# First graph layer of a two-layer GNN kernel: mask laid out per edge, linear part of the leaky logits as product columns, node sums in two halves, node map moved behind the turned logits, GpSimd made to wait for the mask

## What is computed

```python
h = relu(layernorm(x));  s_n, v_n = equivariant_layernorm(h)
msg = (s_n, v_n) @ W_src [src] + (s_n, v_n) @ W_dst [dst]       # gathered rows
m1_s, m1_v = tensor_product(msg, rsh, rbf @ W_rbf)              # per edge
a = (m1_s @ W_alpha).reshape(e, 4, 16)
a = where(a > 0, a, 0.2 * a)                                    # leaky
a = sum(a * alpha_dot, axis=-1)                                 # 4 logits of an edge
ex = exp(a - segment_max(a, dst));  alpha = ex / (segment_sum(ex, dst) + 1e-16)
val = gated(m1_s @ Ws_val, m1_v @ Wv_val)
m2 = tensor_product(val, rsh, w2);  h2 = m2 @ W_vlin            # 4 heads
out = node + segment_sum(alpha * h2, dst) @ W_p
```

## Time and profile before

| | |
|---|---|
| median of 3 runs | 10570.75 us (10557.51 to 10588.19) |
| the profiled execution, its own time | 10573.21 us |
| its span, first to last instruction | 10571.2 us |
| busy: PE, DVE, POOL, ACT | 80%, 70%, 59%, 31% |
| mean granted TensorE clock | 0.899 of full speed |

### The profile page before, as it was taken

The page is one execution under the profiler, slowest core; times in us unless marked ns, Lnnn a source line. Parts: engine busy times, 40 slices in busy tenths (PEclk is TensorE's granted clock), DMA queues, the critical chain, the costliest instruction groups (busy, mean ns, idle before and its releaser), DMA issues. The chain is left out here.

```text
span 10571.2 us, 201187 instructions
## 1 busy us (share of the span) xinstructions
PE 8497.0 (80%) x50848; PEld 6425.6 (61%) x50849; DVE 7420.9 (70%) x18020; ACT 3241.5 (31%) x8443; POOL 6191.2 (59%) x6291
## 2 busy tenths in 40 slices
PE   1388888888888888888888888877658888888888
PEld 1277777777777777777777777766433333333335
DVE  2477777777777777777777777666237777777775
ACT  0133333333333333333333333322222222222223
POOL 0266666666666666666666666543007777677774
PEclk9599999999999999999999999888558888889889
DMA  2133333333333333333333333222002222222221
GB/s 35 48 83 81 83 83 81 82 83 82 81 85 81 84 83 81 83 83 82 83 82 82 83 81 83 71 61 52 8 12 57 57 57 58 58 57 57 57 57 48
DMA packets 560992, 725.68 MB, mean 69 GB/s; under 512 B 228019, under 2 KB 334899, under 8 KB 560956
## 3 DMA queue, kind: packets, MB, share of 16 engines
q0 software_dynamic: 225792, 385.65, 16.3%
q1 hardware_dynamic: 335164, 339.61, 12.1%
HBM read 708.76 MB, written 16.06 MB: 69 GB/s over the span
## 5 line engine op out<-in xcount | busy, mean ns | idle before, releaser
L739 PE MATMUL bank_pair<-w_msg,blocks 128*128 128x160 f32 (+1 forms) x15640 | 2420.7, 318 | 768.1 <-DVE blocks L983 768.1
L739 PEld LDWEIGHTS bank_pair<-w_msg,blocks 128*128 128x128 f32 x15640 | 2314.5, 219 | 859.3 <-DVE blocks L983 859.3
L1377 POOL DMA_INDIRECT gotf<-f_tab,idx x1568 | 1712.8, 1092 | 748.5 <-issue 383.9
L697 POOL DMA_INDIRECT got_src<-src_tab,idx x1568 | 1520.4, 970 | 726.6 <-POOL idx L691 368.3
L697 POOL DMA_INDIRECT got_dst<-dst_tab,idx x1568 | 1495.8, 954 | 529.3 <-issue 527.5
L761 PEld LDWEIGHTS bank_pair<-weights_t,product 128*128 128x128 f32 x12896 | 1493.9, 194 | 309.1 <-issue 294.9
L761 PE MATMUL bank_pair<-weights_t,product 128*128 128x128 f32 x12896 | 1570.5, 281 | 8.9 <-ACT weights_t L885 8.2
L1417 PE MATMUL bank_pair<-val,to_node 128*128 128x449 f32 x3136 | 1477.3, 619 | 6.0 <-DVE val L1520 6.0
L706 POOL TENSOR_TENSOR edge<-rbf,y 128x512 f32<-128x512 f32 x391 | 661.1, 1691 | 1244.5 <-PE bank_pair L728 1137.5
L894 ACT ACTIVATE weights<-near,small 128x512 f32<-128x512 f32 x391 | 282.2, 722 | 3014.1 <-DVE small L933 3014.1
L1468 ACT ACTIVATE val<-pre,y_edge 128x160 f32<-128x160 f32 x1568 | 542.9, 417 | 1894.1 <-DVE pre L1508 1894.1
(11 more groups left out here) (267 smaller groups left out, 12953.8 us busy)
## 6 DMA issues: line engine op xcount, KB each, us to landing
rbf<-in_rbf SPq DMA_DIRECT2D x392, 256.0 KB
dst_bc<-in_dst_rows SPq DMA_DIRECT2D x391, 256.0 KB
y<-in_y SPq DMA_DIRECT2D x392, 128.0 KB
y<-in_y SPq DMA_DIRECT2D x392, 96.0 KB
got_src<-src_tab,idx POOLq DMA_INDIRECT x1568
got_dst<-dst_tab,idx POOLq DMA_INDIRECT x1568
gotf<-f_tab,idx POOLq DMA_INDIRECT x1568
rbf<-in_rbf SPq DMA_DIRECT2D x392, 32.0 KB
```

The source lines that it names most:

```text
L697: pool.indirect_dma_start(out=buf[slot][:, t, :], out_offset=None, in_=table[:, :], in_offset=bass.IndirectOffsetOnAxis(ap=idx[slot][:, c: ...
L739: return nc.tensor.matmul(to, blocks[rows, k, P * t:P * t + P], w_msg[rows, c0:c1], start=start, stop=stop)
L1377: pool.indirect_dma_start(out=got[k % 2][:, t, :], out_offset=None, in_=f_tab[:, :], in_offset=bass.IndirectOffsetOnAxis(ap=idx[k % 2][:, ...
```

## The change

The mask no longer exists as a 128 x 512 tensor that is added to the turned logits. `keys` holds for every edge the place of its node within the window (computed once, in the set-up). In step g DVE compares 32 node numbers with the keys (`apart`, 128 x 128), multiplies by LEAST (`bar`), and, once the logits of g are there, adds mask and logits while widening them (`widen`, 128 x 512). This replaces ACT's widening. The turned logits then carry the mask: the maximum is a plain `tensor_reduce` of PSUM, and ACT takes the exponentials from PSUM. `far`, `near`, `dst_bc` and its DMA are gone.

The leaky function is split: 0.2 times the sum over a head is linear, so it becomes four more columns of the message product (`w_msg`, 160 to 164 columns in the pieces for scalars), and only 0.8 relu is multiplied and reduced (`bent`); one small addition joins the two.

On PE the sums over edges run in two halves around the second pair of `weigh`, and `project` follows `spread_logits`. Its result is copied by ACT from PSUM to SBUF (`pick`, four instructions), and `take_window` becomes one DVE instruction that reads SBUF alone. `multiply` is split: the vector part stays ahead of `messages(g, 2)`, the scalar part goes behind it, followed by the mask. The two peak updates (L937, L938) become one. POOL's `combine` of g+1 waits until DVE has made the mask of group g.

```diff
-MSG_COLS = ((0, 160), (160, 288), (288, 384), (384, 544), (544, 672))
+MSG_COLS = ((0, 164), (164, 292), (292, 388), (388, 552), (552, 680))
...
+                    chain.step(dve.tensor_scalar(w_msg[:, c + 160:c + 164], straight[:, 4 * k:4 * k + 4], 0.2, None, ALU.mult))
...
+                    chain.step(dve.tensor_copy(ahead[:], idx_all[:, :, TILES:2 * TILES]))
...
+                    chain.step(dve.scalar_tensor_tensor(keys[:], ahead[:], 2.0 * BLK, keys[:], ALU.mult, ALU.add))
...
# SP
-                    if late:
-                        wait_apart(sp, s["top"], g, s["tick_s"])
-                    load_dst(g, slot)
...
# POOL, combine
                         wait(s["weighed"], g * 4 - 4)
+                        wait(s["masked"], g * 2)
                     pool.tensor_tensor(edge[slot][:], rbf8[slot][:], y8[slot][:], ALU.mult).then_inc(s["scaled"], 1)
...
# PE
-                            pe.wait_ge(s["win_scaled"], g - 2)
-                        sum_products(slot).then_inc(s["window_sum"], 1)
+                            pe.wait_ge(s["picked"], g - 2)
+                        sum_products(slot, 0, 2)
                     if now:
                         pe.wait_ge(s["block_done"], g * 4 + 2)
                         weigh(1, 0)
                         weigh(1, 1)
                     if late:
+                        sum_products(slot, 2, 4).then_inc(s["window_sum"], 1)
                     if mid:
                         pe.wait_ge(s["turned_copied"], turned)
                         pe.wait_ge(s["logit_wide"], g)
-                        spread_logits(other).then_inc(s["logit_turned"], 1)
+                        spread_logits(other, turn_low).then_inc(s["logit_turned"], 1)
+                    if late:
+                        pe.wait_ge(s["sum_copied"], g - 1)
+                        project().then_inc(s["projected"], 1)
...
# ACT
+                def pick():
+                    for h in range(HEADS):
+                        r = slice(BLK * h, BLK * h + BLK)
+                        last = nc.scalar.activation(picked[r, :], win[r, h, :], ACT.Copy)
+                    return last
...
-                        nc.scalar.activation(logits_wide[other][:].rearrange("p t (h n) -> p (t h) n", h=HEADS),
...
                         hold().then_inc(s["sum_copied"], 1)
+                        act.wait_ge(s["projected"], g - 1)
...
+                        pick().then_inc(s["picked"], 1)
...
-                        nc.scalar.activation(weights[:], near[:], ACT.Exp, bias=minus).then_inc(s["weights"], 1)
+                        nc.scalar.activation(weights[:], turn_low, ACT.Exp, bias=minus).then_inc(s["weights"], 1)
...
# DVE
                 def take_window(g):
...
+                    return dve.tensor_tensor(win_scaled[:], picked[:].unsqueeze(1).broadcast_to(by_side),
...
+                def widen(slot, mask):
+                    by_all = [P, TILES, HEADS, BLK]
+                    return dve.tensor_tensor(logits_wide[slot][:].rearrange("p t (h n) -> p t h n", h=HEADS),
+                                             mask[:].unsqueeze(2).broadcast_to(by_all),
+                                             logits[slot][:].unsqueeze(3).broadcast_to(by_all), ALU.add)
+
+                def bar(mask):
+                    return dve.tensor_tensor(mask[:], mask[:], least[:].unsqueeze(2).broadcast_to([P, TILES, BLK]), ALU.mult)
...
-                        multiply(g - 1, other).then_inc(s["product"], 1)
...
-                        dve.tensor_scalar(far[:], dst_bc[other][:], ring[:, at_group(g - 1)], LEAST, ALU.not_equal,
-                                          ALU.mult).then_inc(s["far"], 1)
+                        multiply_vectors(g - 1, other)
                     if now:
                         messages(g, 2)
+                    if mid:
+                        multiply_scalars(g - 1, other).then_inc(s["product"], 1)
+                    if now:
+                        dve.tensor_tensor(apart[:], iota_row[:, 0:BLK].unsqueeze(1).broadcast_to([P, TILES, BLK]), keys_of(g),
+                                          ALU.not_equal).then_inc(s["masked"], 1)
+                        dve.wait_ge(s["masked"], g * 2 + 1)
+                        bar(apart).then_inc(s["masked"], 1)
...
-                        dve.wait_ge(s["projected"], g - 1)
+                        dve.wait_ge(s["picked"], g - 1)
...
                         take_window(g - 2).then_inc(s["win_scaled"], 1)
...
-                        wait_apart(dve, s["logit_turned"], g, s["tick_v"])
-                        dve.tensor_tensor_reduce(out=near[:], in0=turn_low, in1=far[:], scale=1.0, scalar=LEAST,
-                                                 op0=ALU.add, op1=ALU.max, accum_out=top).then_inc(s["top"], 1)
+                        dve.wait_ge(s["logit_turned"], g)
+                        dve.tensor_reduce(top, turn_low, axis=AX.X, op=ALU.max).then_inc(s["top"], 1)
...
-                            last = dve.scalar_tensor_tensor(lg[:, two, :], a, 0.2, rl[:, two, :], ALU.mult, ALU.add)
...
+                        dve.tensor_tensor(lg[:], rl[:], adot[:].unsqueeze(1).broadcast_to([P, TILES, 64]), ALU.mult).then_inc(s["logit_step"], 1)
...
+                        dve.tensor_reduce(bent[:].rearrange("p t h -> p (t h)"), lg[:].rearrange("p t (h c) -> p (t h) c", h=HEADS),
+                                          axis=AX.X, op=ALU.add).then_inc(s["logit_step"], 1)
+                        dve.wait_ge(s["logit_step"], g * 2 + 2)
+                        dve.tensor_tensor(logits[slot][:].rearrange("p (b t) h -> p b t h", b=2), scalars[:, :, :, 160:164],
+                                          bent[:].rearrange("p (b t) h -> p b t h", b=2), ALU.add).then_inc(s["logit"], 1)
+                        dve.wait_ge(s["logit"], g + 1)
+                        dve.wait_ge(s["masked"], g * 2 + 2)
+                        widen(slot, apart).then_inc(s["logit_wide"], 1)
```

More of the change, by code:

```diff
@@ L296, in _ @@
                 chain.step(dve.tensor_tensor(scale4[:], scale4[:], fac4[:], ALU.mult))
+                for k, c in enumerate((by_a, by_c)):
+                    part = slice(64 * k, 64 * k + 64)
+                    chain.step(dve.tensor_tensor(dotted[:, part], w_msg[:, c + 96:c + 160], adot[:], ALU.mult))
+                    chain.step(dve.tensor_reduce(straight[:, 4 * k:4 * k + 4], dotted[:, part].rearrange("p (h c) -> p h c", h=HEADS),
+                                                 axis=AX.X, op=ALU.add))
+                    chain.step(dve.tensor_scalar(w_msg[:, c + 160:c + 164], straight[:, 4 * k:4 * k + 4], 0.2, None, ALU.mult))
                 for k in range(4):
@@ L489, in layer0 @@
 def layer0(nc, ctx, A, K):
[L490 to L491 removed]
+    (ident, iota_row, iota_col, least_bc, idx_all, w_edge, w_msg, w_val, adot, psum, src_tab, dst_tab, peak, sums) = (K[n] for n in (
+        "ident", "iota_row", "iota_col", "least_bc", "idx_all", "w_edge", "w_msg", "w_val", "adot", "psum", "src_tab", "dst_tab",
         "peak", "sums"))
     s = {n: ctx.enter_context(nc.semaphore("l0_" + n)) for n in (
[L494 to L497 removed]
+        "edge0", "edge1", "edge_y0", "edge_y1", "got0", "got1", "indexed", "summed", "scaled",
+        "turned", "turned_copied", "weighed", "block_done", "message", "tanh", "scalars", "picked", "vector",
+        "gated", "logit", "logit_step", "masked", "logit_wide", "geometry", "product", "scaled_y", "sum_copied", "projected",
+        "logit_turned", "top", "highest", "shifted", "peak_kept", "rescale", "weights", "factors",
         "weights_turned", "weights_copied", "window_sum", "win_scaled", "merged", "tick", "tick_s", "tick_v", "tick_a",
         "tick_p", "more_far", "more_spread", "more_top", "more_step", "more_shifted", "more_weights", "more_factors",
[L500 removed]
+        "more_turned", "more_copied", "more_sum", "more_held", "more_projected", "more_picked", "more_scaled", "more_added", "more_rescale", "zeroed", "step", "span", "meta")}
     with ExitStack() as sx:
@@ L520, in layer0 @@
             low = brief("low0", [P, NG_PAD])
+            ahead = brief("ahead", [P, NG_PAD, TILES])
+            ahead_i = brief("ahead_i", [P, NG_PAD, TILES], I32)
+            place_i = brief("place_i", [P, NG_PAD, TILES], I32)
             step_i = brief("step_i", [P, 200], I32)
@@ L536, in _ @@
                 def _(dve):
-                    chain = Chain(dve, s["step"], 22)
+                    chain = Chain(dve, s["step"], 25)
                     chain.begin(0)
@@ L541, in _ @@
                         dve.memset(y8[i][64:96, :], 1.0)
+                    dve.memset(least[:], LEAST)
+                    for i in range(2):
                         dve.memset(product[i][:, :, 0, 96:97], 1.0)
@@ L588, in layer0 @@
         y_edge = [tmp(f"y_edge0{i}", [P, TILES, 5]) for i in range(2)]
-        dst_bc = [tmp(f"dst_bc{i}", [P, GE], I32) for i in range(2)]
         turned_low = tmp("turned_low", [P, GE])
@@ L598, in layer0 @@
```

(24 more changed lines are left out.)

146 lines of the change are left out of this document (68 added, 78 removed).

## The result

The changed kernel takes 10661.49 us, median of 4 runs (10656.25 to 10666.36), against 10568.6 for the kernel before in the same comparison. The ratio is 1.0086, interval 1.0068 to 1.0103. It is slower, by 0.9%, where 4% were forecast. The profiled span is 10664.6 us, 93 above that of before.

A forecast was written before the change was run, and what follows sets the result against it. It took one loop through PE and DVE, neither full, as the bound. Groups going from 17.25 to 18.25 us gave +391, set-up +12 and further windows +15: 10571 + 418 = 10989, forecast 10990 us, range 10380 to 11230.

The forecast's parts named there:

- the forecast's own: Range of total time for the forecast as summed, without the rivals: 10700 to 11230 us, chance 0.57.
- The chain: Steps through DVE, PE and ACT from `vec` to the next `vec`: 17.6 us a group against 16.7.
- both holds: In DVE's tail, POOL's two operations hold `take_window`, done at 11.35, and `add_sums`, held to 12.85 us behind `vec`.
- The clock: Slow PE stretches at `turn_weights` and the last tile: 0.65 us a group more, making 18.25 us.
- Two of the prediction's own signs of being right: Steady-part mean clock below 0.94; PE's largest idle time ahead of `turn_weights`, 2 us or more.
- The 3.7: Time of PE's message tiles at full clock in us; they would end at 13.0, leaving PE idle 2.6 us.
- Set-up and further windows: Outside the steady groups: +12 us for set-up operations, +15 us for `pick`, `bar` and `widen` in twelve further windows.
- The lock does not bite: In DVE's tail `take_window` and `add_sums` run free: 15.7 us a group, about 9990 us; chance 0.24 with milder form.
- `take_window` first: In DVE's tail `take_window` gets ahead of POOL: 17.1 us a group, 10450 to 10600 us; chance 0.13.
- A wider loss: Slow stretches hit every group at full price, or widening costs its upper bound: 18.9 us, 11240 us; chance 0.06.

The follow-up runs named there:

- b1: Kernel before plus eight unneeded PE transposes in the idle time ahead of the message tiles: 10412.62 us, 0.9845.
- c1: Changed kernel plus two unneeded maxima in DVE's tail, ahead of the real one: 11216.28 us, 1.06.
- a1: Changed kernel without POOL's wait for the mask: 10660.6 us, 1.0074.
- a3: Changed kernel with `pick` undone, `take_window` again four instructions reading PSUM: 10799.04 us, 1.021.
- a4: Changed kernel with the sums over edges in one piece ahead of the second `weigh`: 11808.54 us, 1.1166.
- a2: Changed kernel with POOL's combine waiting for `raise_peak` of the same step instead of the mask: 10276.41 us, 0.9716.
- a6: Changed kernel with POOL waiting for ACT's release instead of the mask, and DVE's register reads moved ahead of `messages(g, 2)`: 10176.52 us, 0.9623.
- b3: Kernel before with one added wait, POOL's combine behind the release of ACT: 10048.19 us, 0.9502.
- l1: Kernel before with the leaky part of the change alone; mask, sums and waits as before: 11150.07 us, 1.0546.
- b2: Kernel before with one added wait, POOL's combine behind `raise_peak` of the same step: 10113.55 us, 0.9562.
- a5: a2 with the sums over edges in one piece ahead of the second `weigh`: 11180.07 us, 1.0567.

## Why the prediction had the sign and not the size

The sign and the mechanism were right, the size was not: 10990 forecast, 10661 measured, inside the range of 10380 to 11230 but not in the forecast's own.

| step, us behind `vec` | forecast | timeline |
|---|---|---|
| `messages(g, 0)` starts | 3.25 | 3.13 |
| second `weigh` | 4.6 | 4.46 |
| `project` | 8.3 | 8.26 |
| PE's tiles start | 9.35 | 9.72 |
| the mask is there | 9.75 | 9.65 |
| `picked` is there | 10.2 | 10.30 |
| POOL starts | 9.97 | 9.83 |
| `take_window` ends | 11.35 | 11.21 |
| the sums end | 13.05 | 12.83 |
| `turn_weights` | 15.6 | 15.32 |
| next `vec` | 17.6 | 17.24 (17.47 the mean) |

- **The chain.** Each step lies within 0.4 us. The halved sums, `held`, `project`, POOL's start and both holds came as worked out. With the mean group, 17.6 was 0.13 us too long: 51 us.
- **The clock, the step that failed.** "With 0.6 stretches a group that is 0 to 1.0 us, and I take 0.65." The clock of the steady part is 1.00 and the term is 0: 391 x 0.65 = 254 of the 329 us. The number of slow stretches was carried over from `before`, although their cause, one gap of 2.0 us, had been taken away by the change itself. The new gaps are 0.81, 0.25 and 1.67 us. b1 shows that shortening the one gap brings the clock back in `before`, c1 that a gap of 2.55 us in `after` would have cost 0.4 to 0.5 us. The mechanism exists, but at 1.67 us it took nothing. Two of the prediction's own signs of being right failed with this term: a clock below 0.94, and a gap of 2 us or more.
- **Why that gap was short.** Forecast 2.6 us ahead of `turn_weights`, measured 1.67. The tiles start 0.37 us later and take 3.92 instead of 3.7, and the weights come 0.28 us earlier: 0.87 together, all in the same direction. Each was a small error; their sum took the gap to a length at which the clock stayed up. The 3.7 was a misreading: the earlier trace rows has 3.90 for the tiles at full clock.
- **Set-up and further windows.** +27 forecast, +12 of it for the set-up. 3655.9 us of the span lie outside the first layer's first and last `vec`, against 3646.3: about +10. Between them the span grew by 83.8 us, no more than the 86 of the groups, so nothing is left to see of the twelve further windows. The rest, 17 us, and the two terms above make 322 of the 329.
- **Not priced: the register reads.** DVE's `marks_of` between `bar` and `take_window` needs 1.05 to 1.11 us. It put the start of `take_window` at 10.66 where the forecast had 10.25. POOL's edge product held it past that, so it cost the forecast nothing, but it bounded a1, a3 and a4.
- **The rivals.** *The lock does not bite*: it did. With POOL kept away (a2) the group takes 16.5 us and not 15.7, with PE waiting 0.84 us for `msg`; a6, with 333 windows in 5400 us, still takes 16.2. *`take_window` first*: `picked` would have had to be there before POOL's start at 9.83 and came at 10.30, and the register reads behind `bar` stand in its way: a4, whose `picked` comes 1.5 us ahead of POOL's start, still has POOL first. *A wider loss*: it needs a longer gap. c1 lies near its 11240, but 0.93 us of c1's group is added work, so that is no support for it.
- **The view of the whole.** At full clock `before` takes 16.72 us and 0.53 more for the clock; `after` takes 17.47 and nothing more. The change gave 0.75 us to a longer chain and got 0.53 back from the clock. Counted over the groups with and without a slow part it is 16.61 to 17.44, 0.83 given, and 0.62 got back.

What stays open: why a6 is 1.3% slower than b3, though POOL lies in the same place in both; how a6's gain over a2 divides between its two edits; and the stall on the other chip, where a6 is the faster of the two by far.

## What to carry to other kernels

Before an operation is rewritten because it is long, see whether it is held: `far` at 1.42 us needed one wait on POOL, not another mask. Price each gap of PE by itself when a clock term is estimated, and work it out anew from where the gap lies after the change. And a shorter path on DVE is no gain by itself: it can bring two-input operations under POOL's, as l1 did on one chip. A ranking of kernels that lie within a few per cent is one of the chip it was taken on: l1 and a6 changed places on another.

## What the runs showed of the hardware

- Two POOL operations of 1.27 and 1.54 us can cost DVE anything from 0 (a2) over 0.24 + 0.97 (L968 and both L987 in `after`) to 1.08 + 1.33 us (L1016 and L1017 in l1), by their place alone. The held DVE instruction ended 0.02 us (L936 and L938 in b3, 0.16 and 0.21 us by themselves) to 0.42 us (L1017 in l1, 0.55) behind POOL's, always less than it takes by itself.
- POOL is held too: L726, 1.54 us, takes 2.63 us in a1 as L725, beside DVE's L1041 and L1044, and 3.5 us in 118 of its 310 groups. In `before` L706 and L710 take 1.70 and 1.71 us in the mean, in b2 1.27 and 1.54.
- Not only instructions with two tensor inputs are held: `far` has one in SBUF, and takes 1.5 us beside POOL and 0.47 to 0.69 without (`before`, b2).
- The clock by PE's longest gap in a group: 1.12 us 0.99 (b1), 1.67 us 1.00 (`after`), 1.81 us 0.98 (a3), 2.0 us 0.94 (`before`), 2.55 us 0.95 (c1), 3.00 us 0.91 (a5), 3.98 us 0.83 (a4). These are means over the groups. PE's total idle time does not order them: `after` has 2.99 us a group in four pieces at 1.00, `before` 2.3, of which 2.0 in one, at 0.94.
